# Cross attention over 12,544 keys: key gathers in two transfers, score group 6 one chunk ahead, difference of maxima last

## The reference

```python
q = (x_1 @ Wq.T + bq)  # 128 queries, 16 heads of 16
k = (x_2 @ Wk.T + bk)  # 12544 keys
v = (x_2 @ Wv.T + bv)
scores = einsum('bhqd,bhkd->bhqk', q, k) * HEAD_DIM ** (-0.5)
attn = softmax(scores, axis=-1)
out = einsum('bhqk,bhkd->bhqd', attn, v)
```

## Time and profile before

| | us |
|---|---|
| median of 3 runs (947.57 to 948.73) | 948.26 |
| the profiled execution | 944.76 |
| its span | 943.0 |
| PE busy in the span | 899.3 |
| DVE busy | 704.8 |
| ACT busy | 487.5 |
| POOL busy | 300.1 |
| exponent pass, first `scores` to last `values` | 596.5 to 906.0 |

### The profile page before, as it was taken

How to read it: one execution, slowest core, us unless ns; L and a number is a source line. 1 busy time by engine, 2 the same in 40 slices (tenths; PEclk the granted TensorE clock), 3 DMA queues, 4 the chain that set the end, 5 groups by cost and what they waited for, 6 DMA issues and landing times. The chain is left out here.

```text
span 943.0 us, 21457 instructions
## 1 busy us (share of the span) xinstructions
PE 899.3 (95%) x8230; PEld 580.0 (62%) x8230; DVE 704.8 (75%) x1216; ACT 487.5 (52%) x1156; POOL 300.1 (32%) x435
## 2 busy tenths in 40 slices
PE   8999999999999999999999989989999999999987
PEld 5444554455445545567788856666667666776675
DVE  3499888988898889997577448768778788887426
ACT  2543454345434544344583413556667666666742
POOL 5564346434643464445065127201100000000100
PEclk9999999999999999999999979999999999999999
DMA  9467855575356535533300078786666667766000
GB/s 171 171 185 211 250 183 171 143 186 183 104 143 186 180 103 158 132 117 119 134 1 1 1 186 215 203 210 163 163 164 164 163 176 185 177 180 187 5 3 6
DMA packets 103655, 136.33 MB, mean 145 GB/s; under 512 B 64152, under 2 KB 85424, under 8 KB 100880
## 3 DMA queue, kind: packets, MB, share of 16 engines
q1 hardware_dynamic: 99856, 134.22, 52.3%
q10 hardware_dynamic: 3712, 0.92, 0.6%
HBM read 81.48 MB, written 53.07 MB: 143 GB/s over the span
## 5 line engine op out<-in xcount | busy, mean ns | idle before, releaser
L1974 DVE TENSOR_REDUCE mx<-bank 128x1 f32<-128x896 f32 x224 | 232.9, 1086 | 54.6 <-PE bank L1818 53.1
L2035 ACT ACTIVATE p<-bank 128x512 f32<-128x512 f32 x392 | 202.9, 602 | 103.7 <-PE bank L1861 103.4
L704 DVE STREAM_TRANSPOSE ew<-sc 32x896 f32<-32x896 f32 x208 | 229.3, 1102 | 15.3 <-ACT sc L788 7.7
L563 PE MATMUL bank<-Wv,ctxT 128*128 128x512 f32 (+1 forms) x336 | 146.4, 575 | 0.0
L1861 PE MATMUL bank<-home,krows 99*128 99x128 bf16 x1568 | 124.7, 220 | 7.7 <-issue 3.4
L1861 PEld LDWEIGHTS bank<-home,krows 99*128 99x128 bf16 x1568 | 101.3, 98 | 46.4 <-issue 9.9
L1818 PE MATMUL bank<-krows,home 96*128 96x512 bf16 x448 | 123.0, 355 | 1.7 <-DMA krows<-kscr 0.9
L1874 PE MATMUL bank<-p,v 128*32 128x128 f32 x3136 | 108.0, 276 | 3.2 <-issue 3.1
L563 PEld LDWEIGHTS bank<-Wv,ctxT 128*128 128x128 f32 x336 | 63.6, 190 | 71.6 <-issue 64.1
L1874 PEld LDWEIGHTS bank<-p,v 128*32 128x32 f32 x3136 | 80.8, 110 | 31.3 <-ACT p L2035 23.0
L445 POOL CAST kt<-kf 128x512 bf16<-128x512 f32 (+1 forms) x56 | 31.3, 558 | 203.3 <-ACT kf L760 203.3
(11 more groups left out here) (317 smaller groups left out, 1158.1 us busy)
## 6 DMA issues: line engine op xcount, KB each, us to landing
krows<-kscr SPq DMA_DIRECT2D x14, 1536.0 KB, 9.9
krows<-kscr SPq DMA_DIRECT2D x14, 1152.0 KB, 14.7
v<-vscr SPq DMA_DIRECT2D x14, 1004.5 KB, 13.8
vscr<-vpair SPq DMA_DIRECT2D x12, 1004.5 KB, 4.0
kscr<-kt SPq DMA_DIRECT2D x14, 768.0 KB, 3.6
kscr<-kt SPq DMA_DIRECT2D x14, 576.0 KB, 5.1
kscr<-kt SPq DMA_DIRECT2D x14, 512.0 KB, 4.5
ctxB<-ctx SPq DMA_DIRECT2D x56, 112.0 KB, 4.0
```

The costliest lines, as they stand in the source:

```text
L563: ins = pe.matmul(bank[kv_bank(op, s)][:, 0:w * D], turned_context(c)[:, i, k * P:(k + 1) * P], Wv01[:, i, 0:w].rearrange("p w o -> p (w o)"),
L704: dve.transpose(pT0[j * SQ:(j + 1) * SQ, :, :, i * SQ:(i + 1) * SQ].rearrange("m t h q -> m h t q"), rows[:, j]).then_inc(S("turn0"), 1)
L1974: dve.tensor_reduce(mx1[:, c % 2, h:h + 1], psum[:, b:b + 2, :].rearrange("p b n -> p (b n)")[:, 0:CH], AX.X, ALU.max).then_inc(S("smread1 ...
L2035: act.activation(p1[:, g % PR, :], bank[ST1[g % 3]][:], ACT.Exp).then_inc(S("exp1"), 1)
```

## The change

Three edits, all in the second attention.

1. `gather` issues two transfers for each half of a chunk, heads 0 to 7 and heads 8 to 15; a partition's row of 16 KB (12 KB) becomes two of 8 KB (6 KB). Both add to the same semaphore, and S0 waits for the sum.
2. `SPLIT` becomes 7: S6 joins the groups of chunk c + 2. The table is shifted by one place up to S15, so S15 stands at step 3 slot 0 and S0 at step 3 slot 1; step 3 slot 2 is empty; M stays at step 4 slot 1; S6 fills step 6 slot 1. `PRO1` gets one more group, S6 of chunk 1, at its end.
3. POOL's `maximum` writes `dm1` after the last term of `n31` instead of in the middle.

```diff
+        GPARTS = 2
+
         def gather(sp, c, half):
 
-            sp.dma_start(krows[half][0:KROWS, c % R1].rearrange("r h m -> r (h m)"),
-                         kscr[half][c].rearrange("j (d h) b m -> (j d) (h b m)", d=D1)
-                         ).then_inc(S(f"krows{half}_{c % R1}"), 16)
+            for part in range(GPARTS):
+                heads = slice(part * H1 // GPARTS, (part + 1) * H1 // GPARTS)
+                sp.dma_start(krows[half][0:KROWS, c % R1, heads].rearrange("r h m -> r (h m)"),
+                             kscr[half][c].rearrange("j (d h) b m -> (j d) (h b) m", d=D1)[:, heads].rearrange("r h m -> r (h m)")
+                             ).then_inc(S(f"krows{half}_{c % R1}"), 16)
...
-        SPLIT = 6
+        SPLIT = 7
...
         PLAN1 = (
-            (("S6",), ("S7",), ("R",)),
-            (("S8",), ("S9",), ("S10",)),
-            (("S11",), ("S12",), ("S13",)),
-            (("S14",), ("S15",), ("S0",)),
+            (("S7",), ("S8",), ("R",)),
+            (("S9",), ("S10",), ("S11",)),
+            (("S12",), ("S13",), ("S14",)),
+            (("S15",), ("S0",), ()),
             (("S1",), ("M",), ("S2",)),
             (("S3",), ("S4",), ()),
-            (("S5",), (), ()))
+            (("S5",), ("S6",), ()))
...
-                if some(c - 1):
-                    pool.wait_ge(S("f1"), c - 1)
-                pool.tensor_tensor(dm1[:, s], run1[:, 1 - s], run1[:, s], ALU.subtract).then_inc(S("dm1"), 1)
...
                 pool.tensor_tensor(n31[:, 2, 0:H1], neg1[:], n31[:, 1, 0:H1], ALU.subtract).then_inc(S("n31"), 1)
+                if some(c - 1):
+                    pool.wait_ge(S("f1"), c - 1)
+                pool.tensor_tensor(dm1[:, s], run1[:, 1 - s], run1[:, s], ALU.subtract).then_inc(S("dm1"), 1)
...
-                        pe.wait_ge(S(f"krows{half}_{r}"), 16 * (c // R1 + 1))
+                        pe.wait_ge(S(f"krows{half}_{r}"), 16 * GPARTS * (c // R1 + 1))
```

## The result

| | before | after |
|---|---|---|
| median, us (7 runs each, side by side) | 948.26 | 934.63 |
| the profiled execution, us | 944.76 | 932.85 |
| its span, us | 943.0 | 931.1 |

The ratio is 0.9867, with a 95% interval of 0.9829 to 0.9905: faster by 1.3%, about 13 us, where 0.8 us had been forecast. The time lies outside the range that was given.

A forecast was written before the change was run, and what follows sets the result against it. PE, working in 95% of the span, was taken as the bound. The terms -1.7 - 0.4 + 0.2 + 1.1 = -0.8 us took 948.26 to 947.4 us, with a range of 943.5 to 951.0 us.

The forecast's parts named there:

- What bounds the kernel: Second attention: PE works in 95% of the span; its largest wait is M for POOL's last term, 5.0 us.
- M's wait goes: Second attention's loop: M stops waiting for POOL's last term, worth 0.39 us a chunk, at most 3.9 us.
- Where that stall goes: Next chunk's first `scores`: waits for maximum rows take most of M's gain; five of thirteen passes keep some, -1.7 us.
- The ends of the loop: Last chunks: a 0.70 us wait goes, -0.4 us; beginning: S6 of chunk 1 added, +0.2 us.
- S0 comes earlier: Step 3: S0 moves 1.01 us earlier, leaving key rows little cover; late in chunks 11 and 12.
- x = 0.2: Key rows assumed to land 0.2 us later with the split gathers; PE then waits 1.1 us in all.
- x = 0.9: Upper bound: key rows land 0.9 us later with the split gathers; five S0s wait 4.6 us together.
- Two transfers for one: Key gathers: two new boundaries between transfers cost 0 to 0.9 us of landing together; PE's waits priced at +1.1 us.
- (c): Rival: smaller key packets move faster, 26 instead of 15 GB/s, emptying chunk 0's queue sooner; 942.4 us; chance 0.08.
- (a): Rival: key rows turn late as each further transfer costs its boundary in full; +2.7 us, 951.0 us; chance 0.18.

The follow-up runs named there:

- e3: Kernel before with only POOL's `dm1` moved to the end: 945.13 us, ratio 0.9991.
- e2: Kernel before with the new order of the groups alone (`SPLIT` 7, shifted table), whole gathers, `dm1` left in the middle: 944.11 us, ratio 0.9983.
- e7: Kernel after with eight transfers by heads for each half (packets of 2 KB and 1.5 KB): 929.36 us, ratio 0.9824 to before.
- e14: Kernel after with eight transfers by heads for each half and 128 bytes of DRAM padding behind every two heads: ratio 0.9880 to before.
- e15: Kernel before (old order, `dm1` as before) with eight transfers by heads for each half: 935.11 us, ratio 0.9893.
- e1: Kernel before with the key gathers in two transfers for each half, nothing else changed: 938.12 us, ratio 0.9914.
- e8: Kernel before without any key gather from chunk 3 on, computing on the keys of chunks 0 to 2: 938.16 us, ratio 0.9903.
- e12: Kernel before, one transfer for each half, DRAM rows padded so packets are 2 KB and 1.5 KB: ratio 1.0071.
- e4: Kernel after with whole gathers again, keeping the new order and `dm1` last: 944.59 us, ratio 0.9981 to before.
- e16: Kernel after with whole gathers and eight tiny transfers issued ahead of each second half from chunk 3 on: ratio 0.9987 to before.
- e18: Kernel after with sixteen transfers for each half, one head each: ratio 1.0542 to before.
- e5: Kernel after with each half cut by partitions into two transfers of 48 neighbouring rows, packets kept at 16 KB (12 KB): ratio 1.0443 to before.
- e11: Kernel after with one transfer for each half, DRAM rows padded so packets are 2 KB and 1.5 KB: ratio 1.0075 to before.
- e9: Kernel after with two transfers for each half, each taking every second partition, packets kept at 16 KB: ratio 0.9918 to before.

## Why the prediction was wrong, point by point

**What bounds the kernel: one wait was missed.** PE being the bound was right. But I read PE's waits by their named releasers, and the nameless ones ("issue"), 6.5 us in the loop, stood beside them. Only one was looked at, and read rightly as a wait for the maximum rows; the other 4.1 us, the stops for code, were not. The irregular steps of 0.2 to 1.8 us were never set against the queue of instructions.

**M's wait goes: right.** No M in the loop waits for POOL. The 0.39 us a chunk was nearly the 0.45 measured. The share of `dm1` was too high: 0.18 us in the prediction, 0.06 in e3, and e2 didn't need it.

**Where that stall goes: the step failed, by 2 to 3 us.** I let five chunks of thirteen keep the gain, -1.7 us; if all eleven keep 0.45 it is -4.95, and by e7 and e14 against e15, where no code is late, chunks 1 to 11 gain 3.9 to 4.2. Of the ten first `scores` that were to wait for their rows, six do. ACT's copy is anchored behind the four exponents, as I had read:

```profile
805.40 2.06 ACT L2039 ACTIVATE p<-bank 128x512 f32<-128x512 f32 x4 [1.05 <-PE bank L1865]
807.33 0.28 ACT L2030 COPY n3T<-bank 96x128 bf16<-96x128 bf16 x1
```

The copy starts 1.04 us after M, against 0.55 in the earlier trace rows. What I held fixed was the landing of the rows. In the chunks where I saw no cover, SP's three issues and the landing took 3.2 to 4.4 us, under traffic. With the short transfers they take 2.9 us from chunk 2 to 7 and in 9: first `scores` then starts 0.13 to 0.18 us after them without a wait. In e15 (eight parts, old order) the cover is 0.64 to 0.67 us in chunks 2 to 7, and the new order uses 0.5 of it. In chunks 11 and 12, where the rows still take 3.5 and 3.8 us, first `scores` waits 0.45 and 0.72 us, as I had said.

**The ends of the loop: the tail had the wrong sign.** Forecast -0.4; the last period went from 20.81 to 21.95 us, +1.1, because the third maximum row now meets a code packet. All twelve others in the new order have it (22.0 to 22.4 us), and of the old order none (20.8 us in e1, e3, e8, e12, e15). At the beginning, +0.2 was forecast and -0.1 is found at chunk 0's first `values`. That chunk 1's first `scores` would still wait 2 us, which was to be the sign, was wrong: 1.4 us, and 0.2 in e7. It is a weak sign, since with whole gathers that wait is anything from 1.3 to 3.1 us (before, e2, e3, e4, e16).

**S0 comes earlier: right.** S0 of chunks 5 and 11 waited 0.13 and 0.15 us, the other chunks from 2 on had 0.4 to 2.0 us of cover. The sum of waits, 0.3 us, is less than the 1.1 of x = 0.2, since the last landing came 0.5 us earlier in the median, not 0.2 later. (For x = 0.9 the covers as listed add up to 4.4 us over six S0s, not 4.6 over five; no bound moves by that.)

**Two transfers for one: the term that decided, and the step that failed most.** I bounded it by the landing of the keys alone, +0 to +4.6 us with +1.1 in the sum, and weighed only whom the keys serve. Who shares the engines with them wasn't asked. Measured: -8 us alone (e1), -11 us on top of the order (0.9867 against e4's 0.9981, of some 945; two different comparisons), where PE's stops for code and the late maximum rows shrink. That fewer bytes in a packet don't speed the keys up by much was right (15.8 against 14.7 GB/s), and the reason that I gave, the shape and not the size, doesn't hold fully: at 2 KB in eight transfers the median reaches 24.4 GB/s, the mean packet (114 ns) 18.

**The rivals.** (c), at 0.08, had the right place in part, chunk 0's stall, by a rate of 26 GB/s that didn't come, and no rival had the code. (a), the Trainium skill's "DMA: Bandwidth & Descriptors", section "Rules for kernel authors", with at least 1 MiB for a transfer: here 768 KB instead of 1,536 is faster, and 192 KB at least as fast; only at 96 KB does the cost of issuing decide (e18). The Trainium skill's 2.0 us in "Anatomy of one DMA", which that section measured on transfers issued by GpSimd and not by SP, are not seen here as a cost paid for each transfer in sequence: the sixteen of e7 have landed 13.4 to 15.1 us after the first issue, the two of before after 14.8 to 15.8.

**The order, once more.** Alone it is worth 1 us (e2, 0.9983) and not 5, although the shortest chunk is 0.45 us shorter, since code stalls and the tail take it back. With the stalls gone, e15 against e14 gives 2.7 us on one chip, with four runs each and their intervals overlapping.

## What to carry to other kernels

Look at PE's waits that the profile puts down to "issue", and set them beside the last landing of what the instruction needs and beside the instruction queue's packets: a long unrolled PE program fetches its own code over the DMA engines, three packets in 21 us here, and large gathers make it late. Cut large background transfers into several (here up to eight of 192 KB; at sixteen, issuing took as long as the landing), and not each onto a block of neighbouring partitions (e5). And when an edit of transfers is priced, ask not only who waits for these bytes but who else uses the engines: here the three small maximum rows and PE's code.

## What the runs showed of the hardware that I had not expected

- PE's code comes in 16 KB packets, each 0.9 to 1.4 us (one 1.75) of one DMA engine in the loop before, one for every 127 pairs of weight load and matmul. Where it came too late in the kernel before, PE went on 1.46 to 1.55 us after the packet's end.
- The number of transfers, with the same bytes, moved the start of those packets from 3.1 to 0.9 us late.
- The rate of 2 KB packets depends on how a transfer walks over the partitions: 24.4 GB/s in the median (18 by the mean) with one packet for each partition (e7, e14), 13.1 with eight for each (e11). Transfers over 48 neighbouring partitions had 16 KB packets of 1.21 us in the median and a tenth of 1.97 us or more; every second partition gave 1.05 (e5, e9). Both are open.
